# A four-layer graph network on one core: the ring of gathered rows in the max pass goes from 16 slots to 32

## What is computed

```python
def _L2_gnn_ref(h, w, src, dst, W1, b1, W2, b2, U1, c1, U2, c2):
    msg_in = jnp.concatenate([h[src], h[dst], w[:, None]], axis=1)
    msg = jax.nn.relu(msg_in @ W1 + b1) @ W2 + b2
    agg = jax.ops.segment_max(msg, dst, num_segments=n)
    agg = jnp.where((deg > 0)[:, None], agg, 0)
    upd_in = jnp.concatenate([h, agg], axis=1)
    return jax.nn.relu(upd_in @ U1 + c1) @ U2 + c2
```

## Time and profile before

| | |
|---|---|
| median of three runs | 6258.78 us (6252.43 to 6262.61) |
| the profiled execution | 6265.11 us, its span 6263.0 us, so 2.1 us lie around the span |
| mean granted clock of PE | 0.948 of full speed |
| PE / DVE / ACT / POOL busy | 85% / 67% / 46% / 28% of the span |
| mix pass, first to last gather | 2530.6 to 3801.4 us |
| max pass, first to last gather | 3928.7 to 5199.6 us |
| mean of one gather on POOL (L548, 1664 of them) | 997 ns |

### The profile page before, as it was taken

How to read it: one execution, slowest core, us unless ns; L and a number is a source line. 1 busy time by engine, 2 the same in 40 slices (tenths; PEclk the granted TensorE clock), 3 DMA queues, 4 the chain that set the end, 5 groups by cost and what they waited for, 6 DMA issues and landing times.

```text
span 6263.0 us, 124636 instructions
## 1 busy us (share of the span) xinstructions
PE 5341.8 (85%) x30743; PEld 3765.3 (60%) x30744; DVE 4168.9 (67%) x12241; ACT 2853.5 (46%) x7039; POOL 1747.1 (28%) x1720
## 2 busy tenths in 40 slices
PE   3677777899999998788888887898999888898988
PEld 2333333788888887444444444666666666777775
DVE  4999999443343334566666667555555556999996
ACT  3566666111111112677677776322222224666664
POOL 1000000000000000566666664666666661000001
PEclk7999999999999999898989887999999999999999
DMA  3333333555555553211111111322222232222220
GB/s 90 106 127 128 128 128 127 198 188 184 179 189 175 210 198 103 56 46 45 45 45 46 45 45 43 92 86 88 87 87 88 87 88 66 106 85 106 85 100 21
DMA packets 395944, 649.07 MB, mean 104 GB/s; under 512 B 99831, under 2 KB 338386, under 8 KB 370639
## 3 DMA queue, kind: packets, MB, share of 16 engines
q1 hardware_dynamic: 330844, 526.22, 25.0%
q0 software_dynamic: 54832, 117.48, 6.9%
q10 hardware_dynamic: 10052, 2.53, 0.2%
HBM read 511.57 MB, written 134.42 MB: 103 GB/s over the span
## 4 chain that ended last, share of the span: by engine, by line
PE 71%; issue 10%; DVE 9%; ACT 5%; ACTq 2%; another core or an unknown queue 1%; DVEq 1%; DMA 1%; POOL 1%; SPq 0%; POOLq 0%
PE ps L1514 19%; PE ps L1570 11%; PE ps L1705 6%; PE ps L1498 5%; PE ps L1624 5%; PE ps L1633 4%; DVE scaled L1099 4%; PE ps L1640 3%; PE ps L1495 3%; PE ps L1626 2%; ACT scaled L1199 2%; PE ps L1627 2%; PE ps L1569 2%; PE ps L1412 2%; PE ps L1647 1%
## 5 line engine op out<-in xcount | busy, mean ns | idle before, releaser
L548 POOL DMA_INDIRECT rg<-tab_L,idxT x1664 | 1658.7, 997 | 3323.7 <-DMA tab_L<-planes 2438.8
L1514 PE MATMUL ps<-planes 128*128 128x384 bf16 (+1 forms) x7350 | 1225.0, 327 | 15.0 <-DVE planes L839 11.6
L1514 PEld LDWEIGHTS ps<-planes 128*128 128x128 f16 (+1 forms) x7350 | 1036.8, 142 | 167.3 <-issue 17.6
L1256 ACT ACTIVATE scaled<-onehot,rg 128x128 f32<-128x128 f32 x2912 | 892.3, 388 | 388.1 <-PE ps L1570 190.6
L1570 PE MATMUL ps<-scaled,rg 128*128 128x512 f32 x1664 | 1020.6, 706 | 0.0
L1705 PE MATMUL ps<-planes,scaled 128*128 128x128 f32 (+1 forms) x4900 | 757.1, 298 | 89.6 <-DVE scaled L1099 89.4
L1569 PEld LDWEIGHTS ps<-rg,onehot 128*128 128x128 f32 x1664 | 337.3, 212 | 745.0 <-issue 390.0
L1099 DVE TENSOR_TENSOR scaled<-scaled,planes 128x256 f32<-128x256 f32 x1225 | 776.7, 716 | 10.5 <-DMA planes<-A_d 7.6
L1199 ACT ACTIVATE scaled<-ps 128x392 f16 x1184 | 588.5, 497 | 411.3 <-PE ps L1498 314.3
L1705 PEld LDWEIGHTS ps<-planes,scaled 128*128 128x128 f32 (+1 forms) x4900 | 628.5, 190 | 209.6 <-DVE scaled L1099 104.6
L826 DVE TENSOR_SCALAR rg<-onehot,planes 128x392 f16<-128x392 f16 x2368 | 723.7, 306 | 0.0
(11 more groups left out here) (256 smaller groups left out, 6239.7 us busy)
## 6 DMA issues: line engine op xcount, KB each, us to landing
planes<-A_d SPq DMA_DIRECT2D x196, 1568.0 KB, 8.2
A_d<-scaled SPq DMA_DIRECT2D x1184, 98.0 KB, 1.7
planes<-rows_d SPq DMA_DIRECT2D x209, 256.0 KB
rg<-tab_L,idxT POOLq DMA_INDIRECT x1664
real_row<-real_d SPq DMA_DIRECT2D x200, 32.0 KB, 4.0
planes<-w_d SPq DMA_DIRECT2D x209, 9.0 KB
tab_L<-planes SPq DMA_DIRECT2D x7, 476.0 KB, 3.1
x_keep<-planes SPq DMA_DIRECT2D x7, 448.0 KB, 3.0
```

The costliest lines, as they stand in the source:

```text
L548: pool.indirect_dma_start(ring[:, q * GROUP + g, 0:width], None, table[:, :], bass.IndirectOffsetOnAxis(idxT[:, at:at + 1], 0)).then_inc(g ...
L1256: last = act.activation(scaled[:, s % 4, m * P:(m + 1) * P], onehot[:, q % 2, g, :], ACT.Copy, scale=ring[:, s, D + m:D + m + 1])
L1514: last = pe.matmul(ps_agg(u), a_blk[n % ABUF][:, 0:w, k], q_rows[l % 2][:, k].rearrange("p t n -> p (t n)"), start=(k == 0), stop=(k == BL ...
```

## The change

POOL no longer calls the common `gather` for the max pass but has a loop of its own, over a ring of 32 places: the first 16 are those of before, the other 16 lie in plane 4 behind `w9`, in what the table has left. A gather of quad T now waits for PE to be done with quad T-8. The places of a quad have eight new semaphores (`max_rows_in`) in place of the four old ones. PE reads the rows from the place of the quad. Since the place and the semaphore are chosen when the program is built, PE's written-out start grows from four quads to eight, and its loop from four quads a pass to eight (25 passes in place of 51). ACT and DVE keep their loops; `stages_of` is put so that the second four quads of PE's start have all their stages. The number of gathers, of matmuls and of all other operations stays.

```diff
+DEEP = 2
@@
+        max_rows_in = [sem(f"max_rows_in{q}") for q in range(DEEP * QPL)]
@@
+        far = pl[:, 4, (1 + QPL + QPL // 2) * 512:(1 + QPL + QPL // 2) * 512 + (DEEP - 1) * RING * D].rearrange("p (r w) -> p r w", w=D)
+        max_rows = [ring[:, s, 0:D] for s in range(RING)] + [far[:, s, :] for s in range((DEEP - 1) * RING)]
@@
-            return q >= lag if isinstance(it, int) else True
+            return q >= lag if isinstance(it, int) and it == 0 else True
@@ POOL
-            gather(L2, tab2, D)
+            pool.wait_ge(tab_written, 16 * CHUNKS * (L2 + 1))
+            for t in range(QUADS):
+                q = t % (DEEP * QPL)
+                pool.wait_ge(mm_done, used(L2, t * GROUP + GROUP - 1 - DEEP * RING))
+                for g in range(GROUP):
+                    at = t * GROUP + g
+                    pool.indirect_dma_start(max_rows[q * GROUP + g], None, tab2[:, :],
+                                            bass.IndirectOffsetOnAxis(idxT[:, at:at + 1], 0)).then_inc(max_rows_in[q], 16)
@@ PE
-            def max_step(it, q):
+            def max_step(it, q, deep=0, h=0):
@@
-                    pe.wait_ge(gathered[q], at * (16 * GROUP) + 16 * GROUP * (L2 * LOOPS + 1))
+                    pe.wait_ge(max_rows_in[h * QPL + q], deep * (16 * GROUP) + 16 * GROUP)
@@
-                        pe.matmul(to, ring[:, s, 0:D], ident, start=True, stop=False)
+                        pe.matmul(to, max_rows[h * RING + s], ident, start=True, stop=False)
@@
-            for q in range(QPL):
-                max_step(0, q)
-            with pe.Fori(1, LOOPS) as i:
+            for h in range(DEEP):
                 for q in range(QPL):
-                    max_step(i, q)
+                    max_step(h, q, 0, h)
+            with pe.Fori(1, LOOPS // DEEP) as i:
+                for h in range(DEEP):
+                    for q in range(QPL):
+                        max_step(i * DEEP + h, q, i, h)
```

More of the change, by code:

```diff
@@ L383, in gnn @@
         w9 = part(4, 0, 1 + QPL, QPL // 2).bitcast(bf16).rearrange("p (q n) -> p q n", q=QPL)
-        sig = scaled
+        far = pl[:, 4, (1 + QPL + QPL // 2) * 512:(1 + QPL + QPL // 2) * 512 + (DEEP - 1) * RING * D].rearrange("p (r w) -> p r w", w=D)
+        max_rows = [ring[:, s, 0:D] for s in range(RING)] + [far[:, s, :] for s in range((DEEP - 1) * RING)]
         def used(p, s):
```

## The result

The changed kernel took 6267.11 us (median of 20 runs, 6259.49 to 6275.18), the kernel before 6252.13 us (median of 20 beside them, 6246.53 to 6263.83): ratio 1.0022, 95% interval 1.0015 to 1.0029. That is 14 us slower by the ratio (15.0 between the medians), small but clear of zero. The profiled execution has a span of 6273.0 us.

What follows compares the result with a forecast made beforehand. PE's semaphore raises, held while POOL gathers, were taken to pace a quad at 6.11 us. 6265.1 + 9 (start) - 3.8 (end) + 0 = 6270.3 us, less 6.3 to the runs' median, gave 6264 us; range 6150 to 6305.

Steps and rivals of the forecast that it cites:

- the hold paces the pass as before: Likeliest case, 0.60: PE's raises stay held while POOL gathers in the max pass, 6.11 us a quad; 6252 to 6280 us.
- the slower rival: Max pass: POOL's longer gather run at the start holds PE's reports 14 to 19 us late; 6274 us, chance 0.10.
- What bounds the kernel: Mix and max pass: PE's raises are held while POOL gathers, so a quad takes 6.11 us instead of 5.16.
- The rows don't come late: Max pass: POOL starts a quad's gathers some 17 us before PE reads them, so more places give PE nothing.
- The start, +9 us with 0 and 14 as ends: Start of max pass: POOL runs on through two former rests, holding PE's reports to about 3994.3; 9 us lost.
- The end, -3.8 us: End of max pass: POOL finishes eight quads ahead, so four more quads take 5.16 instead of 6.11 us.
- the last gather still near 5200 us: Sign expected in the changed kernel's profile: POOL's last max-pass gather near 5200 us, then six or seven prompt quads.
- POOL's loop and PE's branches, 0: Max pass: POOL's period stays 6.11 us; 26 fewer PE branches, 7.8 us, hide behind the hold; 0 us.
- Landing in plane 4: Max pass: half the rows land in another tensor at the same 64 KB a gather; 0 us.
- PE's loop doesn't fit, +43 us: Max pass: PE's doubled loop fetches instructions once in each of 25 passes; 6307 us; chance 0.18 shared with the rows' new place.
- The places are short, 0.22: Max pass: with more places PE goes at its own pace, 5.38 us a quad; 147 us less, 6112 us; chance 0.22.
- The long run holds PE more, 6274 us: Start of max pass: fifth and sixth reports pay for more gathers, hold ends 14 to 19 us late; chance 0.10.

Runs made afterwards that it cites:

- e5: Kernel before, max pass without POOL's gathers; SyncE loads each quad's rows by one plain transfer from fixed rows: 6061.9 us, ratio 0.9697.
- e8: As e5, but POOL makes four real gathers a quad into places that nobody reads: 6248.9 us, ratio 1.0001 to the kernel before.
- e10: Kernel before with POOL allowed two quads ahead of PE instead of four, in mix and max pass: 6544.9 us, ratio 1.1077.
- e1: Changed kernel with POOL's lead put back to four quads (16 gathers), ring of 32 kept: 6294.5 us, ratio 0.9995 to the kernel before.
- e2: Changed kernel with a lead of six quads (24 gathers) instead of eight: 6302.7 us, ratio 1.0009 to the kernel before.
- e3: Changed kernel with a lead of four quads in the pass's first half, eight in the second: 6319.6 us, ratio 1.0028 to the kernel before.
- e4: Kernel before, but from the max pass's fifth quad POOL waits for ACT's count of evacuations instead of PE's: 6363.0 us, ratio 1.0104.
- e6: As e5, but POOL makes four memsets a quad into unused places: 6060.2 us, ratio 0.9696 to the kernel before.
- e7: As e5, but POOL issues four plain 64 KB transfers a quad into unused places: 6058.7 us, ratio 0.9693 to the kernel before.
- e9: Kernel before with POOL allowed three quads ahead of PE instead of four, in mix and max pass: 5916.8 us, ratio 1.0010.
- e12: As e8, but each unread gather takes 8 KB instead of 64 KB: 5883.1 us, ratio 0.9954 to the kernel before.

## Why the prediction was right or wrong

The forecast was 6264 us, with the case that the hold paces the pass as before; the time came out at 6267. In mid-pass and at the end the mechanism stood. That the number is so close is luck. It was a change of +5 us on a base of 6258.8 us, the median of three runs; the median of 20 is 6252.1, and the change is +14 to +15, three times the forecast and what the slower rival had. Two errors cancelled: the base was 6.7 us too high, the change 9 to 10 us too small. Point by point:

- **What bounds the kernel.** Right, and now shown and not only read: without gathers the quad takes 5.16 us (e5), with unread ones 6.1 (e8). "The rows don't come late" held on the chips with the hold; e10 shows where it ends.
- **The start, +9 us with 0 and 14 as ends.** Here is the error: +20.5 us measured, outside both ends. The step that failed is "PE's raises are prompt until 3970.32", carried over to the changed kernel. Two of the four came in POOL's rests: ACT's start at 3966.97 and POOL's restart at 3967.21, ACT's 3955.30 and POOL's 3955.54 are the same release. (The other two, 3960.34 and 3970.32, came among gathers.) I wrote that POOL goes on through both rests and didn't ask what had come through in them. So I had one hold behind four prompt reports, POOL's run ending at 3993.2. After, already the second report is held (3964.33, 13.83 us idle), and the third (3981.99, 14.14 us), and only those before the third paid POOL for more: 40 gathers, not 48. The loss has the size of four quads of gathers run without a rest, 4 x 5.0 = 20 us, but that is no more than a match of numbers. Two things that the sum had at nothing are in it as well, PE's own matmuls 2.1 us apart up to 3981.84 and its clock at 0.50 until 3989; how much of the 20.5 us each takes is open. "For it: hold and gathers end together in every row that I read" stood in the prediction for a rival, and was nearer, though the earlier trace rows and 3964.33 have exceptions.
- **The end, -3.8 us.** Right: seven prompt quads of 5.16 us. But "the last gather still near 5200 us" was wrong by the forecast's own terms: with eight quads of lead it comes four quads earlier against PE. It came at 5187.16, 34.5 us before the last evacuation, where before 13.9 us lay between (5199.56 and 5213.45).
- **POOL's loop and PE's branches, 0.** Near: the median step is 6.08 against 6.09 us, -3 us over the pass. e1, the same code with the old lead, was 3 us below the kernel before with an interval that holds zero, so that the branches gave these 3 us isn't shown.
- **Landing in plane 4, 0.** Right (e1).
- **PE's loop doesn't fit, +43 us.** Refuted. The pages of the four kernels with the doubled loop (the change, e1, e2, e3) have 134 packets on queue 8, that of the kernel before 131: a longer program, fetched once. DMA queues of the changed kernel, 4060 to 5190 us:

```profile
q1 hardware_dynamic: 53805, 50.36, 16.8%
q0 software_dynamic: 23708, 48.61, 14.9%
q14 instruction: 5, 0.04, 0.0%
```

  Queue 8 isn't among them, though the body holds some 600 matmuls and weight loads. The Trainium skill (Runtime: NRT & Kernel Launch, Instruction fetch mechanics) gives PE room for 2048 instructions, and says, without telling the engines apart, that only two pages of 256 are kept. This trace agrees with the first, as far as a loop of some 600 can tell, and not with the second.
- **The places are short, 0.22.** Refuted on the chips that hold: e3 and the change itself are slower for their lead (e2 too, but its interval touches 1), and e4 shows that the hold doesn't come from POOL's wait.
- **The long run holds PE more, 6274 us.** This is what happened, nearly in size: 20.5 - 3.8 - 3.0 = +13.7 us in the trace, +14 in the runs' ratio. I had given it 0.10 and let it decide from 16 us on, with 14 to 19 us at the start. Its way there, a fifth and sixth report that get through and pay for more gathers, is not what the trace shows.
- **What isn't settled.** e3 costs 19.7 us by its trace where the rule gives 16. Why some raises get through a run of gathers and others don't, and why PE itself slows down in a long one, no run tells. Why one chip holds PE's raises while POOL issues indirect transfers and another does not, and whether that is the chip or its state at the time, no run tells.

## What to carry to other kernels

Where idle times end together with another engine's pauses, suspect the pauses, ask for each prompt row whether a pause stood beside it, and price an edit by the pauses that it removes. A deeper prefetch pays only if the consumer waits for its data; here the consumer waited for a word that the prefetching itself kept back, so each quad of lead cost 3 to 6 us. And put a kernel whose bound you can't explain on a second chip before tuning for that bound.

## What the runs showed of the hardware

- While POOL issues indirect transfers back to back, PE's semaphore raises reach ACT, DVE and POOL late: in mid-pass 1.1 us after POOL's last gather has ended (4405.61 to 4406.68), behind long runs 4.1 us (e3, with 17.9 us of idle ACT) and 4.5 us (the change, 3977.45 to 3981.99). Some raises get through among gathers all the same (the change, 3949.80 and 3964.33). Plain transfers from POOL and memsets don't do it (e6, e7). It was so on the chips of the first measurement and of e1 to e8, and absent on the chip of e9 to e12: 6.1 against 5.0 and 5.5 us a quad, some 340 us of 6250.
- In a long run PE's own matmuls come 2.1 us apart (the change, 3974.14 to 3980.44), and PE's clock then stands at 0.50 for 7 us more.
- An indirect transfer of 128 rows costs POOL about 1.0 us and 0.30 us to the next, for 8 KB (1068 ns, e12) as for 64 KB (1073 ns, e9).
- POOL's memsets made DVE's line of 128x512 bf16 slower: 530 ns mean in e6, 332 in e5.
